# Moving two loads, a weight split and the order of the output projection in a six-layer encoder, cross attention and feed-forward kernel

## The reference

```python
def forward(x, Wq, bq, Wk, bk, Wv, bv, Wo, bo, g1, be1, W1, b1, W2, b2, g2, be2, gf, bf):
    x = jnp.flip(x, axis=1)
    for l in range(N_LAYERS):                     # 6 layers, 16 heads of 16
        q = (x @ Wq[l] + bq[l]); k = (x @ Wk[l] + bk[l]); v = (x @ Wv[l] + bv[l])
        a = causal_linear_attn(elu(q) + 1, elu(k) + 1, v)   # chunks of 128 tokens
        x = x + (a @ Wo[l] + bo[l])
        y = x = layer_norm(x, g1[l], be1[l])
        y = gelu(y @ W1[l] + b1[l]) @ W2[l] + b2[l]         # 256 -> 1024 -> 256
        x = layer_norm(x + y, g2[l], be2[l])
    return jnp.flip(layer_norm(x, gf, bf), axis=1)

x = _layernorm(x + encoder(x))
x = _layernorm(x + cross_attention(x, ctx, ctx))
x = _layernorm(x + coupling_network(x))
```

## Time and profile before

| what | value |
|---|---|
| median of 3 executions | 1613.28 us (1612.85 to 1615.44) |
| the profiled execution | 1612.85 us |
| its span, first to last instruction | 1611.1 us |
| mean granted TensorE clock | 0.985 of full speed |
| PE / DVE / ACT / POOL busy | 93% / 80% / 62% / 61% |

### The profile page before, as it was taken

How to read it: one execution, slowest core, us unless ns; L and a number is a source line. 1 busy time by engine, 2 the same in 40 slices (tenths; PEclk the granted TensorE clock), 3 DMA queues, 4 the chain that set the end, 5 groups by cost and what they waited for, 6 DMA issues and landing times.

```text
span 1611.1 us, 38661 instructions
## 1 busy us (share of the span) xinstructions
PE 1504.4 (93%) x16086; PEld 1179.5 (73%) x16086; DVE 1283.0 (80%) x2190; ACT 991.9 (62%) x1608; POOL 989.9 (61%) x704
## 2 busy tenths in 40 slices
PE   4799999999999999999999999999998999999998
PEld 3577888887888878888877888878886566666434
DVE  4778888889888888888888888798775888888456
ACT  3465666666656655666666566656544777777445
POOL 5255767656676566776667666675577466664424
PEclk8799999999999999999999999999998999999999
DMA  6120011100111000210012100102023444443001
GB/s 134 39 63 18 18 25 37 57 25 18 25 45 55 19 18 25 67 38 14 18 25 70 47 9 11 50 16 42 10 51 115 143 142 135 145 134 95 1 1 53
DMA packets 99918, 82.53 MB, mean 51 GB/s; under 512 B 24608, under 2 KB 87968, under 8 KB 99744
## 3 DMA queue, kind: packets, MB, share of 16 engines
q1 hardware_dynamic: 99744, 80.06, 17.5%
HBM read 50.79 MB, written 14.68 MB: 41 GB/s over the span
## 4 chain that ended last, share of the span: by engine, by line
PE 61%; DVE 20%; ACT 9%; POOL 4%; issue 4%; DMA 1%; SPq 1%; DVEq 0%; ACTq 0%; POOLq 0%
PE e_pr L175 6%; PE e_pr L177 5%; PE e_pr L176 5%; PE e_sc L407 4%; PE e_sc L175 4%; PE x_psO L1448 4%; PE e_sc L176 3%; PE e_sc L177 3%; DVE e_qx_lo L898 3%; ACT X L542 3%; DVE e_xT_lo L913 3%; PE e_tr L175 3%; PE e_tr L430 3%; PE e_tr L177 3%; PE e_tr L176 3%
## 5 line engine op out<-in xcount | busy, mean ns | idle before, releaser
L744 POOL TENSOR_TENSOR e_h_lo<-e_h_f,e_h_hi 128x512 fp32r<-128x512 f32 x192 | 256.1, 1341 | 243.8 <-ACT e_h_hi L560 241.7
L559 ACT ACTIVATE e_h_f<-e_pr,e_h_bias 128x512 f32<-128x512 f32 x192 | 131.9, 687 | 274.6 <-PE e_pr L177 269.3
L851 DVE TENSOR_TENSOR e_am<-e_sc,c_amask 128x1024 f32<-128x1024 f32 x192 | 225.7, 1216 | 51.9 <-PE e_sc L407 51.9
L1758 DVE TENSOR_REDUCE x_mx<-x_psS 128x4 f32<-128x1024 f32 x128 | 150.8, 1218 | 28.6 <-PE x_psS L1411 27.7
L175 PE MATMUL e_tr<-e_W_hi,e_h_hi 128*128 128x256 f32 x576 | 165.3, 287 | 7.1 <-DVE X L808 6.2
L175 PE MATMUL e_pr<-e_yT_hi,e_W_hi 128*128 128x512 f32 x384 | 164.9, 429 | 0.0
L176 PE MATMUL e_tr<-e_W_lo,e_h_hi 128*128 128x256 f32 x576 | 162.6, 282 | 0.0
L177 PE MATMUL e_tr<-e_W_hi,e_h_lo 128*128 128x256 f32 x576 | 162.5, 282 | 0.0
L176 PE MATMUL e_pr<-e_yT_lo,e_W_hi 128*128 128x512 f32 x384 | 151.9, 395 | 0.0
L177 PE MATMUL e_pr<-e_yT_hi,e_W_lo 128*128 128x512 f32 x384 | 151.9, 395 | 0.0
L1584 ACT ACTIVATE x_ex<-x_psT 128x1024 f32<-128x1024 f32 x128 | 130.9, 1023 | 26.1 <-PE x_psT L1433 21.3
(11 more groups left out here) (285 smaller groups left out, 4463.3 us busy)
## 6 DMA issues: line engine op xcount, KB each, us to landing
e_raw_m<-in_L_attn_W_dram SPq DMA_DIRECT2D x12, 1024.0 KB, 5.4
x_qs<-query_rows SPq DMA_DIRECT2D x48, 256.0 KB
e_x_raw<-e_x_blocks SPq DMA_DIRECT2D x368, 32.0 KB, 1.9
x_ks<-key_rows SPq DMA_DIRECT2D x48, 128.0 KB, 2.8
query_rows<-x_q_hi SPq DMA_DIRECT2D x16, 256.0 KB, 2.2
query_rows<-x_q_lo SPq DMA_DIRECT2D x16, 256.0 KB, 2.4
x_ctok<-in_ctx_dram SPq DMA_DIRECT2D x8, 256.0 KB, 3.5
x_xo<-in_x_dram SPq DMA_DIRECT2D x8, 256.0 KB, 3.9
```

The source lines that it names most:

```text
L559: act.activation(h_f[:, m % HR, :], ps_pr[m % 2][:, :], ACT.Gelu, bias=h_bias[:, m:m + 1])
L744: pool.tensor_tensor(h_lo[:, m, :], h_f[:, m % HR, :], h_hi[:, m, :].bitcast(F32), ALU.subtract).then_inc(h_lo_done, 1)
L851: dve.tensor_tensor(am[:, s % 2, c, :, :, :], ps_sc[:, :, c * 2 * P:(c + 1) * 2 * P].rearrange("p r (h n) -> p r h n", n=P), amask[:, :].u ...
L1758: dve.tensor_reduce(mx[:, N % 2, :, 0:HG].rearrange("p i (a h) -> p h a i", a=2)[:, pair], ps_s[pair][:, :, :].rearrange("p a (i j) -> p a ...
```

## The change

The change has five parts.

1. On SP, `load_w2(l)` of the steps with q = 0 and l > 0 stands behind `move_x` instead of ahead of it.
2. On SP, the row bo of the next layer is loaded in the step with q = 2, behind `move_x` and bv, instead of in the step with q = 1.
3. The split of W1 goes from the end of the step with q = 3 (ACT) and from the head of the step with q = 0 (POOL, ahead of `rsqrt(1)`) to the middle of the step with q = 0: on ACT behind `ktok`, on POOL behind the lo part of k.
4. On PE, `mlp_up(7)` stands ahead of `project(0)` and `project(1)`; on DVE, `residual(1, 0)` and `residual(1, 1)` stand behind `attn_lo(1)`, each followed by its `spread`.
5. In the last two encoder steps: ACT's `normed(2)` stands behind gelu(3) in the last step too; POOL's `gained(2)`, `gained(1)` and `shifted` stand ahead of `encoder_add(0)`, `x1_norm(0)` and `keys_lo(0)`; DVE's `encoder_stats(0)` stands ahead of `attn_lo(1)`.

```diff
--- before.py
+++ after.py
@@ -235,20 +235,17 @@
 
...
                 more = l < L - 1
-                if l > 0 and q == 0:
-                    sp.wait_ge(w1_lo, l + 1)
-                    load_w2(l)
                 if following:
...
                     load_rows(l, ["g2", "be2"], rows_m, ln2_rows_loaded)
-                if more and q == 1:
-                    sp.wait_ge(xbo_done, NT * l + NT)
-                    load_rows(l + 1, ["bo"], rows_a, bo_loaded)
                 if q < 0:
...
                     load_w2(0)
+                if l > 0 and q == 0:
+                    sp.wait_ge(w1_lo, l + 1)
+                    load_w2(l)
                 if more and q == 0:
...
                     load_attn_weights(l + 1, ["Wq", "Wk", "Wv"], raw_qkv_loaded)
@@ -259,6 +256,8 @@
                 if more and q == NT - 2:
...
                     load_rows(l + 1, ["bv"], rows_a, bv_loaded)
+                    sp.wait_ge(xbo_done, NT * l + NT)
+                    load_rows(l + 1, ["bo"], rows_a, bo_loaded)
                 if more and q == NT - 1:
...
                     load_rows(l + 1, ["g1", "be1"], rows_a, ln1_rows_loaded)
@@ -449,31 +448,24 @@
                         mlp_up(2 + s)
...
                         cross.queries(0, 0, cross.early(2))
-                def project(s):
-                    pe.wait_ge(aT_lo_done, 2 * t + s // 2 + 1)
-                    for c in range(KC):
-                        mm = split3(pe, ps_sc[:, s, 0:D], (aT_hi[:, c, blk(s)], aT_lo[:, c, blk(s)]),
-                                    (hi["Wo"][:, c, :], lo["Wo"][:, c, :]), c == 0, c == KC - 1)
-                    mm.then_inc(wo_full, 1)
-
                 if mlp:
                     mlp_up(6)
+                    mlp_up(7)
                 if attn:
                     pe.wait_ge(o_lo, la + 1)
-                    project(0)
-                    project(1)
-                if mlp:
-                    mlp_up(7)
-                if following and mlp:
-                    pe.wait_ge(qkv_lo, (t + 1) // NT + 1)
-                    pe.wait_ge(xT_lo_done, 2 * t + 4)
-                    pe.wait_ge(gelu_done, FC * u + FC - 1)
-                    qk(0)
-                    pe.wait_ge(gelu_done, FC * u + FC)
-                    qk(1)
-                if attn:
-                    project(2)
-                    project(3)
+                    for s in range(SB):
+                        if following and mlp and s == 2:
+                            pe.wait_ge(qkv_lo, (t + 1) // NT + 1)
+                            pe.wait_ge(xT_lo_done, 2 * t + 4)
+                            pe.wait_ge(gelu_done, FC * u + FC - 1)
+                            qk(0)
+                            pe.wait_ge(gelu_done, FC * u + FC)
+                            qk(1)
+                        pe.wait_ge(aT_lo_done, 2 * t + s // 2 + 1)
+                        for c in range(KC):
+                            mm = split3(pe, ps_sc[:, s, 0:D], (aT_hi[:, c, blk(s)], aT_lo[:, c, blk(s)]),
+                                        (hi["Wo"][:, c, :], lo["Wo"][:, c, :]), c == 0, c == KC - 1)
+                        mm.then_inc(wo_full, 1)
 
...
             cross.queries(0, 1, cross.early(3))
@@ -588,6 +580,11 @@
                     act.wait_ge(raw_qkv_loaded, 48 * (l + 2))
...
                     w_qkv(l + 1)
+                if l > 0 and q == 0:
+                    act.wait_ge(raw_1_loaded, 16 * (l + 1))
+                    act.wait_ge(h_full, FC * u)
+                    w_m("W1", w1_hi, 0)
+                    w_m("W1", w1_hi, 1)
                 if q == NT - 1 and attn:
...
                     act.wait_ge(wo_full, SB * t)
@@ -619,7 +616,7 @@
                         w_m("W1", w1_hi, 1)
...
                         gelu(2 + s)
-                    if s == 1 and u > 0 and attn:
+                    if s == 1 and u > 0:
                         normed(2, u - 1, (q - 1) % NT)
...
                         x_hi(t + 1, s - 1)
@@ -633,15 +630,8 @@
                 if mlp:
...
                     gelu(7)
-                if u == final:
-                    normed(2, u - 1, (q - 1) % NT)
                 if attn:
                     attn_hi(1)
-                if more and q == NT - 1:
-                    act.wait_ge(raw_1_loaded, 16 * (l + 2))
-                    act.wait_ge(h_full, FC * u + FC)
-                    w_m("W1", w1_hi, 0)
-                    w_m("W1", w1_hi, 1)
 
...
             cross.items()
@@ -697,22 +687,17 @@
                     add_row(0, rows_a["bo"], xT_tr, 2, bo_loaded, 16, xbo_done)
...
                     cross.encoder_scale(0)
-                if q == 0 and l > 0:
-                    w_m("W1", w1_hi, l, w1_lo, 0)
-                    w_m("W1", w1_hi, l, w1_lo, 1)
                 if mlp:
                     rsqrt(1, u)
-                    if u == final:
-                        cross.encoder_add(0)
-                    elif u > 1:
+                    if u > 1:
                         gained(2, u - 2, (q - 2) % NT)
                     gained(1, u, q)
-                    if u == final:
-                        cross.x1_norm(0)
-                        cross.keys_lo(0)
-                        gained(2, u - 2, (q - 2) % NT)
                     if u > 1:
                         shifted(u - 2, (q - 2) % NT)
+                if u == final:
+                    cross.encoder_add(0)
+                    cross.x1_norm(0)
+                    cross.keys_lo(0)
                 if attn:
...
                     for c in range(KC):
@@ -721,7 +706,7 @@
                     a.then_inc(k_lo_done, 1)
...
                     w_o(1)
-                if q < 0:
+                if q < 0 or (q == 0 and l > 0):
                     w_m("W1", w1_hi, l, w1_lo, 0)
...
                 if more and q == NT - 2:
@@ -1005,25 +990,21 @@
                     reciprocals(1)
...
                     to_features(1)
-                    residual(1, 0, t, ta, wo_full, xbo_done)
-                    residual(1, 1, t, ta, wo_full, xbo_done)
                 if u == final:
...
                     cross.queries_lo(0, 0, cross.early(2))
+                if u == final - 1:
+                    dve.wait_ge(ln_done[2], final - 2)
+                    cross.encoder_stats(0)
                 if attn:
...
                 if u == final - 1:
-                    dve.wait_ge(ln_done[2], final - 2)
-                    cross.encoder_stats(0)
                     cross.blocks()
                 if attn:
-                    spread(1, 0, t, ta)
-                    spread(1, 1, t, ta)
-                    residual(1, 2, t, ta, wo_full, xbo_done)
-                    spread(1, 2, t, ta)
-                    residual(1, 3, t, ta, wo_full, xbo_done)
-                    spread(1, 3, t, ta)
+                    for s in range(SB):
+                        residual(1, s, t, ta, wo_full, xbo_done)
+                        spread(1, s, t, ta)
                     moments(1, t)
...
```

## The result

The changed kernel takes 1673.71 us (median; 1672.36 to 1675.83), the kernel before 1613.76 us beside it: a ratio of 1.0371, 95% interval 1.0353 to 1.039. The forecast was 1677 us. The span of the profiled execution grew from 1611.1 to 1673.0 us, by 61.9.

The account below looks back on a forecast made before the run. PE bounds the kernel, with 61% of the chain. Plain steps -11.4, bo's load +41, W2's load +16, slow clock +15 and last encoder steps +3 sum to +63.6 us: 1677 us on the median's scale, range 1650 to 1700 us.

Parts of the forecast that it names:

- The bo term: Five steps with q = 2: bo's row lands late behind the copies, ACT waits in normed(2); 8.2 us each, +41 us.
- The clock: PE's granted clock falls after waits: 2 us per step with q = 2, 1 us with q = 0, +15 us.
- Rival A: The two loads cost 57 us in waits, but PE stays at full clock: 1662 us, chance 0.17.
- The W2 term: Five steps with q = 0, l > 0: W2 lands after ACT needs it; +3.2 us each, +16 us.
- the split's place: W1 pieces moved within steps q = 0: normed(1) 1.0 us earlier, residual(2, 2) 1.5 us later, net +0.5 us.
- The pair of 2.9 us: Steps with q = 0: DVE's second e_qx_lo pair, beside POOL's W1 pieces, takes 2.95 us against 1.40 alone.
- rival C: W2 shares its DMA engines with the loads behind it, 5.4 us later, 27 us more: 1704 us, chance 0.08.
- The plain steps: mlp_up(7) ahead of project(0) fills PE's waits: 0.95 us less in each of 12 steps, -11.4 us.
- The last steps: Last two encoder steps: encoder_add(0) 3.5 us later, normed(2) adds up to 2, encoder_stats(0) earlier; net +3 us.
- B: Only bo's load costs; ACT reaches W2 late enough that steps with q = 0 lose nothing: 1656 us, chance 0.08.
- D: Not slower: POOL's add_row finds bo's row in time and only PE's new order counts: 1602 us, chance 0.03.
- E: PE's new order gives nothing, all else holds, 12 us more: 1689 us, chance 0.12.

Follow-up runs that it names:

- the first experiment: The changed kernel with bo's load issued in the step q = 1 again, ahead of the copies of q = 2: 1618.62 us, ratio 1.004.

## Why the prediction was right

**The bo term.** Forecast 41 and clock 10, measured 50.1 in the trace and 0.0331 x 1612 = 53 us by the first experiment. The chain was as the steps had it; the landing was 1.0 us longer than the value I took and inside its ends (the median of all six rose from 3.7 to 4.4). With PE kept busy 39.6 of the 50.1 remain.

**The clock.** 2 us a step with q = 2 was the guess, from a single wait of 3.25 us; measured 2.1. Rival A is out. That for q = 0, 1 us, was not isolated by an experiment.

**The W2 term.** Forecast 16 and clock 5, measured 17.6 in the trace. The sum came out within 3.4 us, the make-up did not. Of the five intervals' +17.6, +3.0 are left with both loads back and -4.2 with the W1 split back as well: W2's place costs 14.6 us in the trace (13.7 to 18.5 by the ratios), where the forecast had 5 x 3.6 = 18, ahead of the slack of `mlp_up(7)`, and the clock; and the split's place 7.2 (0.0042 x 1612 = 7 by the ratios), 1.4 a step, where I had 0.5. That step was mis-sized. The pair of 2.9 us was forecast and came (3.11), and PE's wait at the y transposes grew by the 1.7 us that it is longer. Where the clock stays whole behind that wait the step still loses nothing (last section); what I left out is that this wait, too, can bring the slow clock.

W2 landed in 6.7 us at the median, not 5.5, and there are two parts to that. The issue itself took 1.3 to 1.6 us in three of the five steps and 0.59 in two, where it had taken 0.38; behind the copies Wq had done the same before the change, 1.46 us once and 0.59 in the other four. From the end of the issue W2 landed 5.4 to 6.4 us later in the four steps in which the attention weights follow, 5.0 in the last, where nothing follows, and 5.0 to 5.3 before the change. So rival C is out with its 5.4 us, but a share of it, 0.7 us a step, fits the rows; no run separates it. The attention weights behind it are held up in turn: Wq, issued 0.6 to 1.6 us behind W2, lands within 0.5 us of it, 5.9 us after its own issue where it took 3.0.

On the rows of the pair: by the Trainium skill, SBUF — State Buffer, section "Who interferes with whom", the two engines exclude each other, so that the pair (1.40 us alone) and the four pieces (5.18 us) need 6.6 us one after the other. The trace agrees within 0.3 us: both lie inside the 6.35 us of the four pieces, 484.77 to 491.12. One piece and the second half of the pair in the midst of it:

```profile
486.47 1.71 POOL L667 TENSOR_TENSOR e_W_lo<-e_raw_m,e_W_hi 128x512 fp32r<-128x512 f32 x1
486.98 1.75 DVE L883 SCALAR_TENSOR_TENSOR e_qx_lo<-e_qkT,e_parity,e_qx_hi 128x512 fp32r<-128x512 f32 x1
```

The first half had run to 487.05. The piece, 1.3 us long by itself, then ends at 488.18, and the second half, 0.70 us by itself, at 488.73: each waits for the other's end. What they lost in all (1.7 us on DVE, 1.2 on POOL) fits that. The 4.0 us that I had worked out took a full piece of waiting for each half, but the first half arrives while a piece is already running.

**The plain steps.** -0.95 was forecast for each of twelve; the term is -7.4 instead of -11.4. Six are at about -0.86. The step of mine that failed is what stands ahead of `residual(1, 2)`, said to give back about 0.1 us: it gives back 0.4, as the kernel with PE's half alone shows. I also counted two spreads there as new, which stood there before; only the two residuals, some 0.8 us, are. Five more of the twelve, from the transposition of the step q = 3 to that of q = 0, stand at about -0.47, and at -0.57 to -0.73 where the W1 split is back: they end behind the longer pair. Why they do not reach -0.86 then is open.

**The last steps.** +3 forecast, about +1.3 measured behind the last transposition, the sum of a loss of some 4 us by POOL's order and gains that I did not separate. The same last steps give -0.3 to +4.0 in the other kernels that hold them, so this term can't be told more closely. PE's wait of 3.25 us shrank to 1.81, not to 1.

Rivals B, D and E are out: W2 costs, bo was waited for in all five steps, and the PE order gives 19 us by itself when nothing stands beside it (ratio 0.9885).

That the total came so close, 63.6 us forecast and 61.9 by the spans, is in part luck: the plain steps gave 4.0 us less than forecast, and the steps with q = 0 cost 3.4 us less. The bo term and its clock, the larger part, came out by themselves.

## What to carry to other kernels

A load moved down its queue is priced by what is issued ahead of it, and by the wait in front of that: a line above the copies is early by a whole step, a line below them is late by their issue time and a landing. From where it lands, follow its user's own queue to the engine that sets the end; here POOL was free 15 us before the row landed, and ACT's `normed(2)` came 9 us later. Then add what the bounding engine loses after a wait, and try a reordering of PE apart from the reordering of the engine that feeds it: here one half gained 1.25 us in a plain step and the other gave a third of it back.

## What was not expected of the hardware

The same wait does not always bring the same clock. In the kernel with only W2's load back, PE waits 2.15 or 2.16 us for the same residual in all five steps with q = 0, in u = 4 up to 279.58 and in u = 8 up to 482.97. The windows around these two (columns as above, granted clock ahead of the DMA share) read:

```profile
276.00:282.00 6.00, 3.84 (x57) 3.43 (x56) 6.00 (x9) 2.56 (x4) 6.00 (x5) 0.91 0.00 0
282.00:288.00 6.00, 6.00 (x48) 5.29 (x48) 4.10 (x8) 1.27 (x4) 5.02 (x3) 0.81 0.79 217
```

```profile
479.00:485.00 6.00, 3.85 (x61) 3.44 (x60) 6.00 (x10) 2.56 (x5) 6.00 (x5) 1.00 0.00 0
485.00:491.00 6.00, 6.00 (x70) 4.91 (x71) 5.44 (x13) 2.72 (x6) 5.92 (x4) 1.00 0.73 209
```

The step with the slow stretch is at +0.65 against before, the other at -0.87, like a plain one. So a wait of 2.15 us alone costs nothing there, and the 1.5 us between the two go with the stretch at the lower level (1.2 GHz), the only difference that these rows show. In the kernel with both loads back the slow stretch is there in all five steps (+0.52 to +0.72), in this one in two of five (+0.65 and +0.71; the three without are at -0.83 to -0.87). Busy time of PE is alike in both windows (3.84 and 3.85 us), so the trace doesn't say beforehand which it will be.
